# Two depthwise 3x3x3 convolutions: two of every three 32-channel blocks moved to banded matmuls

## The reference, cut to what matters

```python
def dsconv3d(x, dw_w, dw_b, pw_w, pw_b):
    y = jax.lax.conv_general_dilated(x, dw_w, (1, 1, 1), [(1, 1)] * 3, ...,
                                     feature_group_count=x.shape[1])   # 27 taps, each channel alone
    y = jax.nn.gelu(y + dw_b[None, :, None, None, None], approximate=False)
    y = jnp.einsum('bcdhw,oc->bodhw', y, pw_w) + pw_b[None, :, None, None, None]
    return y
xg = dsconv3d(xg, p['dw1_w'], ...)     # 96 channels, then 96 -> 384
xg = dsconv3d(xg, p['dw2_w'], ...)     # 384 channels, then 384 -> 96
```

## Time and profile before

| | us |
|---|---|
| three timed executions | 19503.61, 19526.52, 19530.97 (median 19526.52) |
| span of the profiled execution, first to last instruction | 19501.0 |
| stage dw1, first DMA issue to that of the next stage | 6021.95 to 6516.09 |
| stage dw2, the same | 6717.23 to 8090.56 |

### The profile page before, as it was taken

One profiled execution on the slowest core, in us unless ns is written; L12 is line 12 of the kernel. 1 busy time (PEld: TensorE's weight loads), 2 busy tenths in 40 slices (PEclk: granted clock), 3 DMA queues, 4 the chain that ended last, 5 costly groups with the idle time before them and its releaser, 6 DMA issues. The chain is left out here.

```text
span 19501.0 us, 270283 instructions
## 1 busy us (share of the span) xinstructions
PE 17868.3 (92%) x76040; PEld 10298.3 (53%) x76040; DVE 16959.5 (87%) x13130; ACT 15757.6 (81%) x24566; POOL 13555.7 (70%) x6692
## 2 busy tenths in 40 slices
PE   8799997899978899898989999999999999989798
PEld 3455553555533344334556666666666666637374
DVE  4799998899977499658989999999999999969798
ACT  7699995899954555566789999999999999935556
POOL 0199990899945489435589999999999999900101
PEclk9899998999989999999999999999999999999899
DMA  5788886788884412366733333333333333252313
GB/s 180 226 246 236 249 241 209 234 246 244 242 240 127 171 72 82 131 244 228 276 144 118 110 112 120 110 111 117 111 112 120 111 113 116 101 169 56 103 51 99
DMA packets 820728, 3086.61 MB, mean 158 GB/s; under 512 B 100022, under 2 KB 123290, under 8 KB 794780
## 3 DMA queue, kind: packets, MB, share of 16 engines
q1 hardware_dynamic: 805532, 3020.15, 48.3%
q10 hardware_dynamic: 13824, 50.34, 0.7%
HBM read 2264.79 MB, written 805.32 MB: 157 GB/s over the span
## 5 line engine op out<-in xcount | busy, mean ns | idle before, releaser
L1587 DVE TENSOR_TENSOR_SCAN l1s_h<-l1s_da,l1s_pd 128x1024 f32<-128x1024 f32 x3072 | 6782.9, 2268 | 233.2 <-PE l1s_pd L1519 135.2
L1630 ACT ACTIVATE l1s_dm<-l1s_dut,l1s_bt 128x384 f32<-128x384 f32 x7424 | 4051.9, 602 | 69.8 <-PE l1s_pd L1519 69.7
L1613 ACT ACTIVATE l1s_da<-l1s_dl,l1s_a 128x1024 f32<-128x1024 f32 x3072 | 3491.6, 1137 | 31.0 <-DVE l1s_h L1587 30.0
L1519 PE MATMUL l1s_pd<-l1s_id,l1s_dm 128*128 128x128 f32 x22272 | 2967.4, 274 | 39.1 <-DVE l1s_h L1587 36.2
L1519 PEld LDWEIGHTS l1s_pd<-l1s_id,l1s_dm 128*128 128x128 f32 x22272 | 2557.4, 142 | 495.0 <-issue 287.8
L1493 POOL TENSOR_TENSOR l1s_pb<-l1s_h,l1s_cc 128x1024 f32<-128x1024 f32 x1024 | 2518.9, 2460 | 91.9 <-DVE l1s_h L1587 76.2
L1497 POOL TENSOR_TENSOR l1s_pa<-l1s_sm,l1s_cc 128x1024 f32<-128x1024 f32 x1024 | 2434.6, 2378 | 0.0
L1530 PE MATMUL l1s_py<-l1s_pb,l1s_both 128*128 128x512 f32 x4096 | 2156.4, 608 | 192.9 <-POOL l1s_pb L1493 192.9
L1488 POOL TENSOR_TENSOR l1s_sm<-l1s_h 128x1024 f32<-128x1024 f32 x928 | 2204.5, 2376 | 120.8 <-DVE l1s_h L1587 120.7
L895 POOL TENSOR_TENSOR dw_acc<-dw_acc,dw_prod 128x961 f32<-128x961 f32 (+3 forms) x704 | 1573.4, 2282 | 907.8 <-ACT dw_prod L848 900.2
L1530 PE MATMUL l1s_py<-l1s_pa,l1s_id 128*128 128x512 f32 x4096 | 2113.4, 598 | 0.3 <-POOL l1s_pa L1497 0.3
(11 more groups left out here) (305 smaller groups left out, 31821.2 us busy)
## 6 DMA issues: line engine op xcount, KB each, us to landing
l1s_cc<-crows SPq DMA_DIRECT2D x1024, 512.0 KB, 3.7
l0sf_cc<-l0crowsf SPq DMA_DIRECT2D x512, 512.0 KB, 5.7
l0sb_cc<-l0crowsb SPq DMA_DIRECT2D x512, 512.0 KB, 5.5
l0sf_cc<-l0crowsf SPq DMA_DIRECT2D x512, 256.0 KB, 7.5
l0sb_cc<-l0crowsb SPq DMA_DIRECT2D x512, 256.0 KB, 7.1
dls<-l1p_dl SPq DMA_DIRECT2D x192, 512.0 KB, 7.0
duts<-l1p_dut SPq DMA_DIRECT2D x64, 1536.0 KB, 6.0
l1s_dut<-duts SPq DMA_DIRECT2D x64, 1536.0 KB, 7.2
```

The source lines that it names most:

```text
L1519: mm = pe.transpose(pd[:, s % 2, blk * 128:blk * 128 + 128], dm[:, rnd % 2, blk, j * 128:j * 128 + 128], idt[:, :])
L1587: dve.tensor_tensor_scan(h[:, s % 4, :], da[:, j, :], pd[:, s % 2, :], 0.0, ALU.mult, ALU.add)\
L1613: act.activation(da[:, j, :], dl[:, half, j, :], ACT.Exp, scale=a[:, HT * half + j, n:n + 1])\
L1630: ins = act.activation(dm[:, rnd % 2, blk, :], dut[:, half, blk, :], ACT.Identity, scale=bt[:, half, blk, n:n + 1])
```

## The change

Both calls of `depthwise` in the first layer are replaced by a new function, `volume_conv`. Channels are now handled in blocks of 32. Of every three blocks, two go through TensorE alone and one goes by taps on the other engines. There is one such step of three blocks for 96 channels and there are four steps for 384.

**The two matmul blocks ("units", `UNITS = 2 * steps`).** A unit is 32 channels of all 32 images. SP loads 8 tiles (`raw`), each of 4 frames by 32 channels on the partitions and 1024 pixels. DVE turns each in blocks of 32x32 (`turn_in`), so that a partition is a frame and a column of pixels, and the free dimension is channel, tile and row. For each channel PE then multiplies by banded matrices that hold the taps in depth and in width. `own` (128x128 weights, up to 256 columns) is done for each of the 3 shifts in height. For the frames that border the other group of four there are 6 more with 32 output partitions and up to 128 columns. The weights are streamed from memory, two channels at a time, into 4 slots. ACT applies bias and Gelu to the 256 results of a channel out of PSUM (`evacuate`), DVE turns the 8 tiles back (`turn_back`), and SP stores them.

**The third block.** Its partitions are 4 volumes by 32 channels, one tile `vol` for the 8 frames of a step. The taps are shared between POOL (with ACT's products) and DVE alone: for an inner frame 1 opening and 11 adds on POOL's side, and 15 taps on DVE; for the two outermost frames 1, 7 and 10.

More of the change, by code:

```diff
@@ L2642, in build @@
     l0_out_proj(nc, x, *ys0, z0, w, xm, n2)
[L2644 to L2649, removed]
+    volume_conv(nc, "dw1", n2, g1, w["dw1_band"], w["dw1_edge"], w["dw1_bias"], w["dw1_taps"], 1, ACT.Gelu)
     hid, g2 = (dram(n, (IMAGES, 3, 128, HW)) for n in ("hid", "g2"))
     l0_expand(nc, g1, w, hid)
-    depthwise(nc, "dw2", 128, lambda i, v: hid[bass.ds(i * FRAMES, FRAMES), v].rearrange("b p n -> p b n"),
-              lambda i, v, f: one(g2[:, v], i * FRAMES + f),
-              w["dw2"], w["dw2_b"], w["ident"], 3, 3, 4, True, ACT.Gelu)
+    volume_conv(nc, "dw2", hid.rearrange("b t p n -> b (t p) n"), g2.rearrange("b t p n -> b (t p) n"),
+                w["dw2_band"], w["dw2_edge"], w["dw2_bias"], w["dw2_taps"], 4, ACT.Gelu)
     x0, x1 = (dram(n, (IMAGES, C, HW)) for n in ("x0", "x1"))
@@ L2739, in arranged, with volume_tables @@
         w[f"skip_{d}"] = pair_tiles(v[f"L0_conv_D_{d}"])
-    w["dw1"] = v["L0_conv_dw1_w"].reshape(C, 1, 27)
-    w["dw1_b"] = column(v["L0_conv_dw1_b"])
+    def volume_tables(taps, offsets):
+        blocks = taps.reshape(-1, 3, 32, 27)
+        steps = len(blocks)
+        cubes = blocks[:, :2].reshape(steps * 2, 32, 3, 3, 3)
+        rows = np.zeros((3, steps * 2, 32, 3, 32, 32), f)
+        for z in range(3):
+            for x in range(3):
+                to = np.arange(max(0, 1 - x), min(32, 33 - x))
+                rows[z][:, :, :, to + x - 1, to] = cubes[:, :, z, :, x, None]
+        rows = rows.transpose(0, 1, 2, 4, 3, 5).reshape(3, steps * 16 * 2, 2, 32, 3, 32).swapaxes(2, 3)
+        band = np.zeros((steps * 32, 4, 32, 2, 3, 4, 32), f)
+        for to in range(4):
+            for of in range(max(0, to - 1), min(4, to + 2)):
+                band[:, of, :, :, :, to] = rows[of - to + 1]
+        flat = blocks[:, 2].repeat(4, axis=0).reshape(steps, 4, 32, 27).reshape(steps, 128, 27)
+        parts = offsets.reshape(steps, 3, 32)
+        last = parts[:, 2].repeat(4, axis=0).reshape(steps, 128, 1)
+        return {"band": band.reshape(steps * 32, 128, 2, 3, 128), "edge": np.stack([rows[2], rows[0]], 1),
+                "bias": np.broadcast_to(parts[:, :2].reshape(1, steps * 2, 32), (128, steps * 2, 32)),
+                "taps": cat([flat, last], 2).swapaxes(0, 1)}
+    for name in ("dw1", "dw2"):
+        for part, table in volume_tables(v[f"L0_conv_{name}_w"], v[f"L0_conv_{name}_b"]).items():
+            w[f"{name}_{part}"] = table
     w["pw1"] = v["L0_conv_pw1_w"].T
     w["pw1_b"] = tiles(v["L0_conv_pw1_b"], 3)
-    w["dw2"] = tiles(v["L0_conv_dw2_w"].reshape(HID, 27), 3)
-    w["dw2_b"] = tiles(v["L0_conv_dw2_b"], 3)
     w["pw2"] = tiles(v["L0_conv_pw2_w"].T, 3)
```

277 lines of the change are left out of this document (added).

## The result

The changed kernel takes 19222.47 us (median of 4 runs, 19219.21 to 19248.37) against 19526.12 for the kernel before. The ratio is 0.9852, with an interval of 0.9838 to 0.9866. It is faster by 304 us. I had forecast 831 us, and the time lies outside my range.

What follows compares the result with a forecast made beforehand. PE bounded the old kernel; afterwards POOL (181 us a step) and DVE (178) would. With start, boundaries and end, dw1 takes 231 and dw2 805, saving 831 us: 18,700, range 18,640 to 18,950.

Steps and rivals of the forecast that it cites:

- The joint bounds POOL and DVE: In both depthwise stages after the change, POOL (181 us a step) and DVE (178) set the pace together.
- the DMA term: Per step, 39 MB at 333 or 242 GB/s take 118 or 162 us, below POOL's 181.
- 2.8 us after its issue in a quiet queue: Landing time assumed for output stores at a unit boundary, putting the 8 turns back at 13.5 us.
- Rival 3: SP's full queue binds: stores land after 18.0 us, 8 turns back take some 40, +27 us a unit, 18,970; chance 0.06.
- Its sign: The mark of SP's list as the bound: DVE waits for DMAs in turns both ways.
- The turns: DVE's 32 turns a step at 1.17 us each, 37.5 us, with bounds of 0.75 and 3.38 us a turn.
- rival 1: DVE's turns are dear: at 2.4 us each DVE has 216 us a step, +170, 18,870; chance 0.16.
- my 5: POOL's standstill at each of the 8 inner unit boundaries: about 3 us, taken as 5 with small losses.
- 22 and 23: Ends of each depthwise stage: 22 us before POOL starts, 23 us for last merges, turns back, landing and stage change.
- 25.5 us: Added to the forecast span of 18,670 because the earlier median lay that far above the profiled span, giving 18,695.
- a matmul's price: PE's matmuls at 0.227 and 0.125 us: 1.43 us a channel, 46 us a unit, covered by POOL's 90.6.
- rival 2: PE at 1.2 GHz: 92 us a unit, ACT's evacuations wait for PE mid-unit (its sign), 18,800; chance 0.12.

Runs made afterwards that it cites:

- e1: The split: changed kernel with each tile DMA issued as four of 32 partitions, outermost dimension 32; 18756.8 us, ratio 0.9608.
- e4: Changed kernel with each tile DMA cut into two halves of 512 pixels, still 4 entries outermost; 19222.52 us.
- e5: Changed kernel with each tile DMA cut into two by pairs of frames, 2 entries outermost; 20343.9 us.
- e3: Changed kernel without weight loads after the first four pairs of channels of a stage (wrong results); 19134.35 us.
- e2: Changed kernel with the turned buffers laid out tile by tile, turn stride 128 B instead of 1 KB; 19220.4 us, ratio 0.9849.
- e12: Changed kernel, tile DMAs unsplit, with turns of only 16 of 32 image rows (wrong results); 19207.68 us.
- e9: e1 with turns of only 16 of 32 image rows in both directions (wrong results); 18740.14 us, ratio 0.9594.
- e8: e1 without the 6 edge matmuls of each channel (wrong results); 18756.44 us.
- e7: e1 with POOL's share of an inner frame 12 adds instead of 11, one tap fewer on DVE; 18796.77 us, ratio 0.9632.
- e11: e1 with both ACT's first evacuation after 16 list entries instead of 9 and POOL's share 12; 18772.0 us, ratio 0.9611.
- e10: e1 with ACT's first evacuation of a unit after 16 list entries instead of 9; 18747.44 us, ratio 0.9599.

## Why the prediction was wrong

The direction was right and the size was not. The joint bounds POOL and DVE hold only after the split: in the changed kernel neither is one. Of the forecast 831 us, 304 came. The split gives 466 more, and that leaves about 61.

**The step that failed: the DMA term.** I divided 39 MB a step by 333 or 242 GB/s, rates of stretches with DMA shares of 0.93 and 0.89, and got 118 to 162 us, under POOL's 181. The tiles are 25.2 of the 39 MB and go at 105 GB/s: 240 us a step for them alone, 290 us measured for the whole step. "2.8 us after its issue in a quiet queue", which I used for the stores, is the same mistake: it was the landing of a transfer of another shape. Both rows were right, and neither was of a DMA with 4 entries outermost. The diff shows that shape ("8 tiles, each of 4 frames by 32 channels on the partitions"), and no transfer of the earlier trace rows has it. Both ends of my bound were below POOL's 181, and none of them came from a transfer of another shape. The runs show it from four sides: e1 undoes the shape and gains 466, e4 keeps it and changes nothing, e5 makes it worse and loses 1121 against e4, e3 takes the other bytes away and gains 88.

**Rival 3 had the place and not the mechanism.** I wrote that 8 turns back through 3 buffers would take 40 us if stores landed late, and they do take 40 us (7212.68 to 7252.88). Its sign came too: DVE waits for DMAs in the turns both ways, 191.0 us and about 200 in dw2. But I asked for a queue full of transfers, with landings after 18 us, and argued against it with the mean load, which is the failed term again. Its 18,970 lies 250 us below the measured time, since I had the price for the turns back alone. SP's list does fill up in the changed kernel, since single DMA issues take up to 8.2 us (0.58 at the median for the tile loads of dw2), but as a consequence: e4 with more issues costs nothing.

**The turns, a term mis-sized.** I took 1.17 us from the merges. They take 1.90 to 1.97 (e2, and the groups above), so DVE has 141 + 32 x 1.93 = 203 us a step and not 178 (the groups of dw2 sum to 201, and the profile counts 196 busy, without overlaps). My bounds 0.75 and 3.38 held it, and rival 1, dear turns, is right in kind at a lower price than its 2.4 us. In the changed kernel the turn's price costs nearly nothing (e12: 15 us). Once the DMAs are right it makes DVE the bound: in e1 a unit takes 102 us (POOL's bursts start at 6935.23 and 7037.28) instead of 95.6. At a boundary the 8 turns back take 19.5 us instead of 13.5, which is most of what the gap of 11.6 us has over my 5. POOL's first and last burst in dw2, in e1 and then in e9:

```profile
6509.92 15.68 POOL L1214 TENSOR_TENSOR dw_acc<-dw_acc,dw_prod 128x992 f32<-128x992 f32 x7 [25.21 <-ACT dw_prod L1162]
...
7241.97 74.05 POOL L1214 TENSOR_TENSOR dw_acc<-dw_acc,dw_prod 128x992 f32<-128x992 f32 x33 [12.30 <-ACT dw_prod L1162]
```
```profile
6514.70 15.70 POOL L1216 TENSOR_TENSOR dw_acc<-dw_acc,dw_prod 128x992 f32<-128x992 f32 x7 [19.10 <-ACT dw_prod L1162]
...
7211.88 74.07 POOL L1216 TENSOR_TENSOR dw_acc<-dw_acc,dw_prod 128x992 f32<-128x992 f32 x33 [5.42 <-ACT dw_prod L1162]
```

From the first add to the last, e1 takes 806 us and e9, with turns at my price, 771, where I had 8 x 90.6 + 7 x 5 = 760. So the turns are 35 of the 46 us that e1 is over there. The start and the end of dw2 were 27 and 28 us, against 22 and 23. By stages e1 is 72 us over the forecast (247.3 + 860.8 against 231 + 805), by the median 61. That the second is smaller is luck. I had added 25.5 us for the median over the profiled span, and that is the spread of the runs before (the profiled one was the fastest, 19503.61 us, 2.6 over its span). e1's profiled run is within 1 us of its median, and the rest of the program is 14 us longer in it than in the profile before.

**PE, mis-sized and harmless.** I read a matmul's price from a row whose count is of records, and every f32 matmul leaves two. The changed kernel shows it: 9 matmuls a channel, 256 channels, 4608 records in dw2. The rows of before had shown it as well: 12 pairs of 6 x 18 + 2 x 12 matmuls are 1584, and the earlier trace rows has 3168. In e1, right behind a unit boundary and at full clock, the timeline has these rows. Twelve records are the six edge matmuls of a channel; six are its two closing own ones and the opening one of the next:

```profile
7041.64 1.54 PE L1116 MATMUL dw_pc<-dw_xin,dw_wb 128*128 128x248 f32 x6
7043.11 0.84 PE L1124 MATMUL dw_pc<-dw_xin,dw_we 128*32 128x128 f32 x12
7043.87 1.54 PE L1116 MATMUL dw_pc<-dw_xin,dw_wb 128*128 128x248 f32 x6
```

A channel starts every 2.23 us (7041.64 to 7043.87), 71 us a unit instead of 46. The lower clock of rival 2 came too. The granted clock was 0.76 in dw2, a mix of 2.4 and 1.2 GHz, after 0.98 before. PE had pauses in it, 196.4 us for weights, 176.5 for ACT and 108.5 for DVE's turns. A channel took 669.92/256 = 2.62 us of busy PE, 84 us a unit. In e1, with 617.28 us busy in dw2 at clock 0.85, a unit is 77 us. There PE doesn't set the time, as e8 shows. In the changed kernel ACT's evacuations do wait for PE in the middle of a unit, rival 2's sign, but PE waits for its weights first; what its clock adds there no run shows.

**What held.** POOL's sum, 180 us a step against 181. Taps, merges and products at their old prices. Evacuations at 0.42 us (106.7/256) against 0.4. The order of events at the boundary: the last add, merges, turns back, ACT's first evacuation, POOL's gap. l0_expand kept its length within 3 us. Of a slip in my sums, rival 1's 216 us should be 218, which changes nothing.

**What stays open.** Why a turn costs 1.90 us: its hops or the operation. About 11 us of dw2 between first and last add, and 10 at its ends. Moving a tap to POOL gained nothing, with 40 us lost in e7 and no clear difference in e11, although DVE is the bound by e9. In e11 POOL waits 57.0 us for products in dw2 (111.2 in e1), and DVE 28.2 for POOL before merges (11.0 in e1); what else eats the tap that was moved, no run separates. A single DMA for a tile with the 32 channels outermost on both sides would tell whether the four issues cost anything; it wasn't tried. Of the versions that leave nothing out e1 and e10 are the fastest, and they can't be told apart.

## What to carry to other kernels

Before dividing bytes by a rate, read the outermost dimension of the DMA's access pattern, and ask whether the rate's row had the same. A partition dimension put together from a short outer part (4 frames) and a longer inner part is better issued as one DMA for each outer entry; here that gave 466 us. The signs in this profile were a DMA share stuck near 0.25 (0.13 in e5) with engines waiting for landings, and equal tiles that landed equal times apart. And where two engines wait for each other at a unit's end, moving work from one to the other can lengthen the row, as in e7.

## What the runs showed of the hardware that I had not expected

- 512 KB took 5.0 us with 4 entries outermost (105 GB/s, share 0.25, four packets under way at once). With 2 entries outermost it was 52 GB/s and share 0.13, with two packets at once. In four DMAs of 32 entries the first loads of dw1 ran at 247 GB/s with share 1.00.
- A packet of 4096 B took 159 ns with two or four engines at work, 26 GB/s for one engine, and 271 ns at the median in those 8 us at share 1.00.
- DVE turned 128x1024 f32 in 32x32 blocks in 1.90 us with POOL idle, the same with hops of 128 B and of 1 KB, and 128x512 in 1.00. Beside POOL's adds the 1024 took 2.04 us at most.
- A one-input f32 multiplication SBUF to SBUF of 128x1024, with the hops of the turns, took 1.03 us alone and up to 3.22 beside POOL's adds, and single adds took up to 3.17 us beside it.
- At a granted clock of 1.00, twelve records of f32 matmuls with 32 output partitions and 124 to 128 columns took 0.84 us, 0.07 each, and six with 128 output partitions and 248 to 256 columns took 1.54 us, 0.257 each. Every f32 matmul left two records.
